# A fused embedding, attention and expert kernel: DVE's statistics of a tile behind the maximum of their unit, and one product in the next unit

## The chip, the core and the metric

The kernel runs on one core of a Trainium2 chip. The metric is the device time of one execution in microseconds (us). Three runs of the kernel before took 1317.76, 1317.83 and 1319.64 us.

The engines are named as in the profile: PE multiplies matrices, DVE, ACT and POOL work on vectors, SP issues transfers. Each runs its own list of instructions in order. They wait for one another only through semaphores, and what stands behind a waiting instruction on the same engine waits too.

## The reference, cut to what matters

Tokens (8 sequences of 1024) are hashed into 2-, 3- and 4-grams and embedded; the embedding is projected to 128 channels (`h`). Then comes attention with three branches, and then 32 experts. The change is in the attention:

```
out_cross = ln(softmax(q k_down^T) v_down)      # 512 keys: the sequence halved by a convolution
out_dot   = ln(softmax(q k^T) v)                # 1024 keys
out_cos   = ln(softmax(qn kn^T / t) v)          # 1024 keys, q and k divided by their norms
gate = softmax(concat(out_cross, out_dot, out_cos) gw + gb)
h    = h + gate0 * out_cross + gate1 * out_dot + gate2 * out_cos
```

Each `ln` subtracts a mean, divides by a standard deviation, multiplies with a weight `g` of 128 channels and adds a bias `b`. Behind this the 32 experts take the 256 tokens each that the router's softmax ranks highest, and their weighted results are added up.

## The kernel before

The attention is cut into units. A unit is one branch of one tile of 128 tokens: 8 sequences of 8 tiles with 3 branches are 192 units, and unit s belongs to the cross branch when s mod 3 is 0, to the dot branch when it is 1, to the cosine branch when it is 2. Every engine walks the same loop over s (`for s in range(N + TAIL)`), each with work of several units at once. In pass s:

- PE multiplies queries and keys of unit s into `scores`, turns the exponentials of unit s - 1 (line 610, "turned" or "mixed" <- probs) and multiplies the turned ones of unit s - 2 with the values (line 629, `mixed`). Before and behind this it computes the "items" that a table places in the pass.
- DVE copies the result of unit s - 3 out of PSUM (line 868, `o`), copies items out, and takes the row maximum of unit s (line 862, `neg_max`).
- ACT copies items, takes the exponentials of unit s (line 1019) and copies what PE turned (line 1028, `pT`).

Between these stands the work of a tile n, whose units are 3n to 3n + 2:

- pass 3n + 5: DVE's statistics (`tile_stats`, three `bn_stats` and three `bn_aggr`, lines 875 and 880), and POOL's `tile_rstd` (lines 1118 to 1126), whose third instruction waits for them;
- pass 3n + 6: DVE's `tile_gate_logits` (lines 886 to 891), which waits for `tile_rstd`;
- pass 3n + 7: ACT's exponential of the gate (line 1009), at the head of its pass; DVE's `tile_gate`: three small instructions (lines 896 to 900) and three products `u` = o * gate_r * ln_g (line 905);
- pass 3n + 8: POOL's `tile_sum` (lines 1132 to 1144): five instructions, of which the first two need the gate, and the third and later ones the products `u`. The last writes `h1`;
- pass 3n + 9: DVE's `tile_h1_stats` (lines 913 and 916), which waits for `h1` and stands ahead of the logits of the tile n + 1;
- pass 3n + 10: POOL's `tile_rstd2`, and in pass 3n + 11 ACT's `tile_x2`.

The items prepare the next sequence. Their places in the 24 passes of a sequence stand in tables: `FIRST` and `SECOND` for sequences 0 and 1, `STEADY` for sequences 2 to 6, `LAST` for 7. `|` parts what stands ahead of PE's turning from what stands behind its product with the values; a `+` means the next sequence. Two entries of `STEADY` matter here, at places 10 and 16 of 24:

```
"xT1+ | route1-"       # place 10: transposes the normalised tokens of the next sequence's second half
"k_c0+ | gram1++"      # place 16: transposes the normalised cosine keys
```

Both need POOL and another engine two passes ahead. For `xT1+`, POOL's pass of place 8 has `token_rstd` (lines 1099 to 1104), and ACT's pass of place 8 ends with `normalise` (line 1033, `xn`), which waits for it. For `k_c0+`, POOL's pass of place 14 has `cos_norm` (lines 1108 and 1111), and DVE's pass of place 15 ends with `cos_scale` (lines 794 to 801), which waits for it. In POOL's list both stand behind `tile_sum` and `tile_rstd` of their pass, since 8 and 14 are 2 modulo 3. POOL also issues the gathers of the embeddings (line 1090), three for an item, four passes ahead of it.

Of the kernel before, what the change touches and what calls it, by code (L numbers as in the profile page):

```python
# [5 lines left out]
ALU = mybir.AluOpType  # L6
# [9 lines left out]
B, S, C = 8, 1024, 128  # L16
# [19 lines left out]
BR = 3  # L36
# [71 lines left out]
N = B * UNITS  # L108
# [32 lines left out]
def items_at(s):  # L141
    return (*PLACED.get((s, 0), ()), *PLACED.get((s, 1), ()))
# [32 lines left out]
def build_program(nc, x_tok, emb, weights, cols, rows, consts, cand_bits, w_up, b_up, w_down, out):  # L175
    table = nc.dram_tensor("token_table", (TOK, XW), F32, kind="Internal").ap()
    with ExitStack() as ctx:
# [3 lines left out]
        def sem(name):  # L181
            return ctx.enter_context(nc.semaphore(name))
# [3 lines left out]
        def asb(name, shape, dt=F32):  # L186

            return attn.enter_context(nc.sbuf_tensor(name, shape, dt))
# [80 lines left out]
        o = asb("o", [P, 4, BR, VW])  # L269
# [10 lines left out]
        gate_r = asb("gate_r", [P, 2, 3])  # L280
        u = asb("u", [P, 2, BR, C])
# [54 lines left out]
        gate_r_ok = sem("gate_r_ok")  # L336
        scale_ok = sem("scale_ok")
        u_ok = sem("u_ok")
        z_g = sem("z_g")
        h1_ok = sem("h1_ok")  # L340
# [22 lines left out]
        def R(name):  # L363
            return row[:, ROW[name][0]:ROW[name][1]]
# [291 lines left out]
        def _(dve):  # L656
# [202 lines left out]
            def maxima(n):  # L859
                width = SD if n % BR == 0 else S  # L860
                dve.wait_ge(scored, n + 1)
                dve.tensor_reduce(neg_max[:, n % 4:n % 4 + 1], scores[:, (n % 2) * S:(n % 2) * S + width], AX_X,  # L862
                                  ALU.max, negate=True).then_inc(maxed, 1)

            def output(n):
                t, br = n // BR, n % BR
                dve.wait_ge(pv_done, n + 1)
                dve.tensor_copy(o[:, t % 4, br, :], mixed[:, 0:VW]).then_inc(o_ok, 1)  # L868

            def tile_stats(n):  # L870

                m = n % 2
                dve.wait_ge(o_ok, BR * n + BR)
                for br in range(BR):
                    last = dve.bn_stats(st[:, m, br, :], o[:, n % 4, br, 0:C])
                last.then_inc(o_stats, 1)
                dve.wait_ge(o_stats, n + 1)
                dve.nop(nofuse=True)
                for br in range(BR):
                    last = dve.bn_aggr(mv[:, m, br, :], st[:, m, br, :])  # L880
                last.then_inc(o_mv, 1)
# [11 lines left out]
            def tile_gate(n):  # L893
                m = n % 2
                dve.wait_ge(gate_ok, n + 1)
                dve.reciprocal(gate_inv[:, m:m + 1], gate_sum[:, m:m + 1]).then_inc(gate_c, 1)
                dve.wait_ge(gate_c, n + 1)
                dve.scalar_tensor_tensor(out=gate_r[:, m, :], in0=gate_e[:, m, :], scalar=gate_inv[:, m:m + 1],
                                         in1=rstd[:, m, :], op0=ALU.mult, op1=ALU.mult).then_inc(gate_r_ok, 1)
                dve.tensor_scalar(gate[:, m, :], gate_e[:, m, :], gate_inv[:, m:m + 1], None, ALU.mult).then_inc(scale_ok, 1)  # L900
                dve.wait_ge(gate_r_ok, n + 1)
                if n >= 2:
                    dve.wait_ge(h1_ok, n - 1)
                for br in range(BR):
                    last = dve.scalar_tensor_tensor(out=u[:, m, br, :], in0=o[:, n % 4, br, 0:C],  # L905
                                                    scalar=gate_r[:, m, br:br + 1], in1=R("ln_g")[:, br * C:(br + 1) * C],
                                                    op0=ALU.mult, op1=ALU.mult)
                last.then_inc(u_ok, 1)

            def tile_h1_stats(n):  # L910
                m = n % 2
                dve.wait_ge(h1_ok, n + 1)
                dve.bn_stats(st2[:, m, :], h1[:, n % NT, :]).then_inc(st2_ok, 1)
                dve.wait_ge(st2_ok, n + 1)
                dve.nop(nofuse=True)
                dve.bn_aggr(mv2[:, m, :], st2[:, m, :]).then_inc(mv2_ok, 1)
# [5 lines left out]
            for s in range(N + TAIL):  # L922
                if 0 <= s - 3 < N:
                    output(s - 3)
                if s % BR == 2 and 0 <= s - 5 < N:
                    tile_stats((s - 5) // BR)
                for k in PLACED.get((s - 1, 1), ()):
                    evict(k)
                if s < N:
                    maxima(s)  # L930
                for k in PLACED.get((s, 0), ()):
                    evict(k)
                if s % BR == 0 and 0 <= s - 9 < N:
                    tile_h1_stats((s - 9) // BR)
                if s % BR == 0 and 0 <= s - 6 < N:
                    tile_gate_logits((s - 6) // BR)
                if s % BR == 1 and 0 <= s - 7 < N:
                    tile_gate((s - 7) // BR)
                for where in range(2):
                    for k in PLACED.get((s - 1 - where, where), ()):  # L940
                        if ITEMS[k][0] == "route":
                            route_probs(*ITEMS[k][1:])
                for k in items_at(s + 1):
                    name, seq, j = ITEMS[k]
                    if name == "k_c" and j == 0:
                        cos_scale(seq)
# [135 lines left out]
        def _(pool):  # L1082
# [30 lines left out]
            def tile_rstd(n):  # L1113

                m = n % 2
                pool.wait_ge(exped, BR * n + BR)
                s = exp_sum[:, n % 4, :]
                pool.tensor_tensor(sum_sq[:, m, :], s, s, ALU.mult).then_inc(rstd_g, 1)
                pool.wait_ge(rstd_g, n * 3 + 1)
                pool.nop(nofuse=True)  # L1120
                pool.tensor_scalar(var_eps[:, m, :], sum_sq[:, m, :], LN_EPS, None, ALU.mult).then_inc(rstd_g, 1)
                pool.wait_ge(rstd_g, n * 3 + 2)
                pool.wait_ge(o_mv, n + 1)
                pool.tensor_tensor(var_eps[:, m, :], var_eps[:, m, :], mv[:, m, :, 1], ALU.add).then_inc(rstd_g, 1)
                pool.wait_ge(rstd_g, n * 3 + 3)
                pool.tensor_tensor(rstd[:, m, :], var_eps[:, m, :], m_half[:, 0:BR], ALU.pow).then_inc(rstd_ok, 1)

            def tile_sum(n):

                m, t, b = n % 2, n % NT, n // NT  # L1130
                pool.wait_ge(scale_ok, n + 1)
                pool.tensor_tensor(zb[:, m, :, :], R("ln_b").rearrange("p (i c) -> p i c", c=C),  # L1132
                                   gate[:, m, :].unsqueeze(2).to_broadcast([P, BR, C]), ALU.mult).then_inc(z_g, 1)
                pool.wait_ge(z_g, n * 4 + 1)
                pool.tensor_tensor(zb[:, m, 0, :], zb[:, m, 0, :], h[:, (b % 2) * NT + t, :], ALU.add).then_inc(z_g, 1)
                pool.wait_ge(z_g, n * 4 + 2)
                pool.wait_ge(u_ok, n + 1)
                pool.tensor_tensor(u[:, m, :, :], u[:, m, :, :], zb[:, m, :, :], ALU.add).then_inc(z_g, 1)  # L1138
                pool.wait_ge(z_g, n * 4 + 3)
                pool.tensor_tensor(u[:, m, 0, :], u[:, m, 0, :], u[:, m, 1, :], ALU.add).then_inc(z_g, 1)  # L1140
                pool.wait_ge(z_g, n * 4 + 4)
                if t % 4 == 0 and b > 0:
                    pool.wait_ge(h1_stored[t // 4], b * 16)
                pool.tensor_tensor(h1[:, t, :], u[:, m, 0, :], u[:, m, 2, :], ALU.add).then_inc(h1_ok, 1)
# [33 lines left out]
            for s in (2, 3):  # L1178
                for k in items_at(s):
                    if ITEMS[k][0] == "gram":  # L1180
                        gathers(*ITEMS[k][1:])
            for s in range(N + TAIL):
                if s % BR == 2 and 0 <= s - 8 < N:
                    tile_sum((s - 8) // BR)
                if s % BR == 2 and 0 <= s - 5 < N:
                    tile_rstd((s - 5) // BR)
                if s % BR == 1 and 0 <= s - 10 < N:
                    tile_rstd2((s - 10) // BR)
                for k in items_at(s + 2):
                    name, seq, j = ITEMS[k]  # L1190
                    if name == "xT":
                        token_rstd(seq, j)
                    if name == "k_c" and j == 0:
                        cos_norm(seq)
                for k in items_at(s + 4):
                    name, seq, j = ITEMS[k]
                    if name == "gram" and j < NT:
                        gathers(seq, j)
# [644 lines left out]
```

## Time and profile before

| | |
|---|---|
| median of three runs | 1317.83 us |
| the profiled execution | 1317.56 us |
| its span in the trace | 1315.6 us |
| PE busy | 1090.7 us (83%) |
| DVE busy | 832.2 us (63%) |
| POOL busy | 802.2 us (61%) |
| ACT busy | 677.2 us (51%) |
| attention, from the first maximum of scores to the last statistics of `h1` | 72.6 to 999.6 us |

The profiled execution took 1.96 us more than the span that the trace shows of it, and 0.27 us less than the median. A timeline row gives start and duration of an instruction, or of several equal ones in a row (x3), and in brackets how long the engine had been idle and who ended this. Instructions of DVE overlap a little, so that a group can be shorter than its members together.

### The profile page before, as it was taken

How to read it: one execution, taken by the hardware profiler on the slowest of the kernel's cores; microseconds unless marked ns; L12 is line 12 of the kernel's file. 1: busy time of each engine (PE TensorE's matmuls, PEld its weight loads, DVE VectorE, ACT ScalarE, POOL GpSimd, SP SyncE). 2: the span in 40 equal slices, each digit the busy share in tenths (PEclk: the TensorE clock that was granted, in tenths of full speed). 3: DMA queues.
4: the chain of work that ended last, by engine and by line, in shares of the span. 5: the costliest groups of instructions: out<-in, count | busy, mean ns of one | idle time of the engine just before them, and what ended most of it. 6: DMA issues, size and time to landing. Idle time of an engine off the chain costs nothing. (4 is left out here: it accounts for less than half of the span.)

```text
span 1315.6 us, 23060 instructions
## 1 busy us (share of the span) xinstructions
PE 1090.7 (83%) x7468; PEld 959.8 (73%) x7468; DVE 832.2 (63%) x2531; ACT 677.2 (51%) x1702; POOL 802.2 (61%) x1252
## 2 busy tenths in 40 slices
PE   3679999999999999999999999999982248876752
PEld 3569888888888988898888889888881126664541
DVE  4356777787776867777686777776675874421110
ACT  0346656666575665656566665656562543421210
POOL 5356775777467658756765775554553006778784
PEclk9889999999999999999999999999996557898885
DMA  2010001000001001100100110000002002444442
GB/s 94 22 31 25 21 20 31 25 26 18 20 24 32 27 12 43 30 9 26 31 24 14 43 29 9 11 9 19 11 9 71 0 0 48 78 94 78 83 68 23
DMA packets 49082, 42.47 MB, mean 32 GB/s; under 512 B 6728, under 2 KB 44488, under 8 KB 48840
## 3 DMA queue, kind: packets, MB, share of 16 engines
q0 software_dynamic: 18432, 22.04, 8.9%
q1 hardware_dynamic: 30536, 19.00, 4.7%
q8 instruction: 61, 1.00, 0.3%
q14 instruction: 53, 0.43, 0.1%
HBM read 27.38 MB, written 13.63 MB: 31 GB/s over the span
## 5 line engine op out<-in xcount | busy, mean ns | idle before, releaser
L629 PE MATMUL mixed<-v,pT 128*128 128x132 f32 x2560 | 320.6, 276 | 1.4 <-DVE o L868 1.4
L629 PEld LDWEIGHTS mixed<-v,pT 128*128 128x128 f32 x2560 | 302.7, 190 | 3.0 <-issue 2.6
L1090 POOL DMA_INDIRECT gram<-in_emb,ids x192 | 192.2, 1001 | 66.2 <-issue 52.7
L862 DVE TENSOR_REDUCE neg_max<-scores 128x1 f32<-128x1024 f32 (+1 forms) x192 | 199.0, 1036 | 52.0 <-PE scores L431 51.6
L1019 ACT ACTIVATE probs<-scores,neg_max 128x1024 f32<-128x1024 f32 (+1 forms) x192 | 186.7, 972 | 60.4 <-DVE neg_max L862 60.3
L1028 ACT ACTIVATE pT<-turned 128x512 f32<-128x512 f32 x211 | 125.3, 594 | 64.9 <-PE turned L610 64.5
L610 PE MATMUL turned<-con,probs 128*128 128x128 f32 x844 | 124.8, 276 | 20.0 <-ACT probs L1019 8.1
L1132 POOL TENSOR_TENSOR zb<-row,gate 128x384 f32<-128x384 f32 x64 | 54.7, 854 | 142.0 <-DVE gate L900 141.6
L429 PE MATMUL scores<-k_hi,q_hi 128*128 128x512 f32 x320 | 135.9, 425 | 2.3 <-DVE q_lo L764 2.3
L431 PE MATMUL scores<-k_hi,q_lo 128*128 128x512 f32 x320 | 126.2, 394 | 0.0
L430 PE MATMUL scores<-k_lo,q_hi 128*128 128x512 f32 x320 | 126.1, 394 | 0.0
L1779 POOL DMA_INDIRECT out_h<-yw,slots x64 | 102.2, 1597 | 36.5 <-issue 15.5
L610 PEld LDWEIGHTS turned<-con,probs 128*128 128x128 f32 x844 | 96.8, 141 | 36.8 <-ACT probs L1019 16.7
L1770 POOL DMA_INDIRECT xg<-token_table,slots x64 | 64.9, 1015 | 94.2 <-DVE slots L1632 75.0
L1729 ACT ACTIVATE hid<-scores,bup 114x256 f32<-114x256 f32 (+1 forms) x96 | 38.6, 472 | 130.8 <-PE scores L1476 130.8
L905 DVE SCALAR_TENSOR_TENSOR u<-o,gate_r,row 128x128 f32<-128x128 f32 x192 | 99.1, 570 | 0.0
L868 DVE COPY o<-mixed 128x132 f32<-128x132 f32 x192 | 54.9, 286 | 54.0 <-PE mixed L629 53.8
L1476 PE MATMUL scores<-xT,wu 128*114 128x256 f32 (+1 forms) x192 | 64.2, 483 | 24.0 <-DVE xT L1647 17.7
L1028 ACT ACTIVATE pT<-mixed 128x512 f32<-128x512 f32 x109 | 64.9, 595 | 28.9 <-PE mixed L610 28.9
L1654 DVE TENSOR_SCALAR yw<-mixed,xg 128x128 f32<-128x128 f32 x64 | 19.5, 346 | 90.1 <-PE mixed L1487 75.2
L610 PE MATMUL mixed<-con,probs 128*128 128x128 f32 x436 | 66.4, 275 | 11.6 <-ACT probs L1019 7.1
L1138 POOL TENSOR_TENSOR u<-u,zb 128x384 f32<-128x384 f32 x64 | 64.5, 1008 | 15.1 <-DVE u L905 13.7
(300 smaller groups left out, 2426.4 us busy)
## 6 DMA issues: line engine op xcount, KB each, us to landing
wd<-in_w_down SPq DMA_DIRECT2D x32, 171.0 KB
token_table<-w SPq DMA_DIRECT2D x16, 320.0 KB, 2.4
out_h<-h SPq DMA_DIRECT2D x16, 256.0 KB, 2.3
gram<-in_emb,ids POOLq DMA_INDIRECT x192, 2.6
wu<-in_w_up SPq DMA_DIRECT2D x8, 170.5 KB, 4.0
w<-in_weights SPq DMA_DIRECT2D x1, 1174.0 KB, 7.4
xg<-token_table,slots POOLq DMA_INDIRECT x64, 2.8
out_h<-yw,slots POOLq DMA_INDIRECT x64, 3.4
```

The lines of the kernel that those rows point to most:

```text
L429: pe.matmul(dst, lhs[0], rhs[0], start=first_one, stop=False)
L430: pe.matmul(dst, lhs[0], rhs[1], start=False, stop=False)
L431: return pe.matmul(dst, lhs[1], rhs[0], start=False, stop=last_one)
L610: last = pe.transpose(dst[:, j * P:(j + 1) * P], probs[:, n % 2, half * 512 + j * P:half * 512 + (j + 1) * P], ident)
L629: last = pe.matmul(mixed[:, 0:VW], pT[:, n % 2, j * P:(j + 1) * P], vals, start=(j == 0), stop=(last_half and j == half * 4 + 3))
L862: dve.tensor_reduce(neg_max[:, n % 4:n % 4 + 1], scores[:, (n % 2) * S:(n % 2) * S + width], AX_X, ALU.max, negate=True).then_inc(maxed, 1)
L905: last = dve.scalar_tensor_tensor(out=u[:, m, br, :], in0=o[:, n % 4, br, 0:C], scalar=gate_r[:, m, br:br + 1], in1=R("ln_g")[:, br * C:(b ...
L1019: act.activation(probs[:, n % 2, 0:width], scores[:, (n % 2) * S:(n % 2) * S + width], ACT.Exp, bias=neg_max[:, n % 4:n % 4 + 1], accum_ou ...
L1028: act.activation(pT[:, n % 2, half * 512:half * 512 + 512], shared_bank(TURNED_ON[n, half]), ACT.Identity).then_inc(pT_ok, 1)
L1090: pool.indirect_dma_start(gram[:, t % 4, g, :], None, emb[g], bass.IndirectOffsetOnAxis(ap=ids[:, s, t, g:g + 1], axis=0)).then_inc(gather ...
L1770: pool.indirect_dma_start(xg[:, e % XB, half, :], None, table, bass.IndirectOffsetOnAxis(ap=slots[:, k:k + 1], axis=0)).then_inc(x_in[e % ...
L1779: pool.indirect_dma_start(rows_out, bass.IndirectOffsetOnAxis(ap=slots[:, k:k + 1], axis=0), yw[:, e % EB, half, :], None, compute_op=ALU. ...
```

## The change

On DVE, `tile_stats` moves from ahead of the maximum of its pass (and of the items of the pass before) to behind it. Of the three products `u`, the first two stay behind the gate in pass 3n + 7, and the third moves into pass 3n + 8, behind the statistics of the next tile. Each product now signals `u_ok`, and POOL waits for three signals a tile. On POOL, `tile_rstd` of the tile n and `tile_sum` of the tile n - 1, which stand in one pass, change places.

```
@@ vector: tile_gate ends behind tensor_scalar(gate...)
-                dve.wait_ge(gate_r_ok, n + 1)
-                if n >= 2:
-                    dve.wait_ge(h1_ok, n - 1)
-                for br in range(BR):
-                    last = dve.scalar_tensor_tensor(out=u[:, m, br, :], in0=o[:, n % 4, br, 0:C],
-                                                    scalar=gate_r[:, m, br:br + 1], in1=R("ln_g")[:, br * C:(br + 1) * C],
-                                                    op0=ALU.mult, op1=ALU.mult)
-                last.then_inc(u_ok, 1)
+            def tile_gain(n, br):
+                m = n % 2
+                if br == 0:
+                    dve.wait_ge(gate_r_ok, n + 1)
+                    if n >= 2:
+                        dve.wait_ge(h1_ok, n - 1)
+                dve.scalar_tensor_tensor(out=u[:, m, br, :], in0=o[:, n % 4, br, 0:C],
+                                         scalar=gate_r[:, m, br:br + 1], in1=R("ln_g")[:, br * C:(br + 1) * C],
+                                         op0=ALU.mult, op1=ALU.mult).then_inc(u_ok, 1)
@@ vector: the loop
-                if s % BR == 2 and 0 <= s - 5 < N:
-                    tile_stats((s - 5) // BR)
                 for k in PLACED.get((s - 1, 1), ()):
                     evict(k)
                 if s < N:
                     maxima(s)
+                if s % BR == 2 and 0 <= s - 5 < N:
+                    tile_stats((s - 5) // BR)
...
                 if s % BR == 1 and 0 <= s - 7 < N:
                     tile_gate((s - 7) // BR)
+                    tile_gain((s - 7) // BR, 0)
+                    tile_gain((s - 7) // BR, 1)
+                if s % BR == 2 and 0 <= s - 8 < N:
+                    tile_gain((s - 8) // BR, 2)
@@ gpsimd: tile_sum
-                pool.wait_ge(u_ok, n + 1)
+                pool.wait_ge(u_ok, n * BR + BR)
@@ gpsimd: the loop
+                if s % BR == 2 and 0 <= s - 5 < N:
+                    tile_rstd((s - 5) // BR)
                 if s % BR == 2 and 0 <= s - 8 < N:
                     tile_sum((s - 8) // BR)
-                if s % BR == 2 and 0 <= s - 5 < N:
-                    tile_rstd((s - 5) // BR)
```

On DVE, in the passes of places 7 to 9 of a sequence, there stood before (`gate_r` and `gate` are the end of `tile_gate`, `st<-o` and `mv<-st` the statistics, `neg_max` the maxima of places 8 and 9, `st<-h` and the `mv` behind it `tile_h1_stats`):

```order
L900 TENSOR_SCALAR gate<-gate_e,gate_inv 128x3
L905 SCALAR_TENSOR_TENSOR u<-o,gate_r,row 128x128 x3
L868 COPY o<-mixed 128x132
L875 BN_STATS st<-o 128x6 x3
L880 BN_AGGR mv<-st 128x2 x3
L862 TENSOR_REDUCE neg_max<-scores 128x1
L868 COPY o<-mixed 128x132
L862 TENSOR_REDUCE neg_max<-scores 128x1
L913 BN_STATS st<-h 128x6
L916 BN_AGGR mv<-st 128x2
L886 TENSOR_TENSOR logit<-o,rstd 128x3x3
```

In the changed kernel there stands at the same place of DVE:

```order
L900 TENSOR_SCALAR gate<-gate_e,gate_inv 128x3
L908 SCALAR_TENSOR_TENSOR u<-o,gate_r,row 128x128 x2
L868 COPY o<-mixed 128x132
L862 TENSOR_REDUCE neg_max<-scores 128x1
L875 BN_STATS st<-o 128x6 x3
L880 BN_AGGR mv<-st 128x2 x3
L908 SCALAR_TENSOR_TENSOR u<-o,gate_r,row 128x128
L868 COPY o<-mixed 128x132
L862 TENSOR_REDUCE neg_max<-scores 128x1
L915 BN_STATS st<-h 128x6
L918 BN_AGGR mv<-st 128x2
L886 TENSOR_TENSOR logit<-o,rstd 128x3x3
```

The maximum of place 8 moved ahead of the statistics, and the third product behind them. Nothing was added or taken away.

On POOL, in the pass of place 8, there stood before (`zb` to `h` is `tile_sum`, `sum_sq` to `rstd` is `tile_rstd`, and the last row is the first of `token_rstd`):

```order
L1132 TENSOR_TENSOR zb<-row,gate 128x384
L1135 TENSOR_TENSOR zb<-zb,h 128x128
L1138 TENSOR_TENSOR u<-u,zb 128x384
L1140 TENSOR_TENSOR u<-u 128x128
L1144 TENSOR_TENSOR h<-u 128x128
L1118 TENSOR_TENSOR sum_sq<-exp_sum 128x3
L1121 TENSOR_SCALAR var_eps<-sum_sq 128x3
L1124 TENSOR_TENSOR var_eps<-var_eps,mv 128x3
L1126 TENSOR_TENSOR rstd<-var_eps,m_half 128x3
L1099 TENSOR_SCALAR shift<-mv 128x4
```

In the changed kernel (lines from here on are 6 higher):

```order
L1124 TENSOR_TENSOR sum_sq<-exp_sum 128x3
L1127 TENSOR_SCALAR var_eps<-sum_sq 128x3
L1130 TENSOR_TENSOR var_eps<-var_eps,mv 128x3
L1132 TENSOR_TENSOR rstd<-var_eps,m_half 128x3
L1138 TENSOR_TENSOR zb<-row,gate 128x384
L1141 TENSOR_TENSOR zb<-zb,h 128x128
L1144 TENSOR_TENSOR u<-u,zb 128x384
L1146 TENSOR_TENSOR u<-u 128x128
L1150 TENSOR_TENSOR h<-u 128x128
L1105 TENSOR_SCALAR shift<-mv 128x4
```

The two groups changed places; what comes behind both kept its place. At place 14 it is the same, with `cos_norm` behind both groups:

```order
L1132 TENSOR_TENSOR rstd<-var_eps,m_half 128x3
L1138 TENSOR_TENSOR zb<-row,gate 128x384
L1141 TENSOR_TENSOR zb<-zb,h 128x128
L1144 TENSOR_TENSOR u<-u,zb 128x384
L1146 TENSOR_TENSOR u<-u 128x128
L1150 TENSOR_TENSOR h<-u 128x128
L1114 TENSOR_TENSOR norm<-norm,p_half 128x16
```

This is the changed kernel; before, `cos_norm` followed `tile_rstd` there.

## Rows read from the trace of the kernel before

**Rows 1.** Busy time by stage: stretch, us, then each engine, PEclk, DMA share, GB/s.

```profile
79.60:89.70 10.10, 6.91 (x26) 5.29 (x25) 5.07 (x8) 3.41 (x7) 7.97 (x8) 0.50 0.19 50
600.00:800.00 200.00, 192.98 (x1412) 175.95 (x1411) 150.40 (x442) 124.79 (x306) 140.14 (x243) 1.00 0.10 28
```

**Rows 2.** PE's waits from 60 to 1005 us: total, times, longest.

```profile
PE turned L610 <- ACT probs L1019: 8.1, 9, 1.9
PE mixed L610 <- ACT probs L1019: 7.1, 9, 1.1
```

**Rows 3.** Timeline of DVE, units 128 and 129: start us, us, instruction [idle before].

```profile
699.27 1.72 DVE L905 SCALAR_TENSOR_TENSOR u<-o,gate_r,row 128x128 f32<-128x128 f32 x3
...
701.23 0.68 DVE L875 BATCH_NORM_STATS2 st<-o 128x6 f32<-128x128 f32 x3
...
702.24 1.19 DVE L862 TENSOR_REDUCE neg_max<-scores 128x1 f32<-128x1024 f32 x1
...
704.18 0.28 DVE L913 BATCH_NORM_STATS2 st<-h 128x6 f32<-128x128 f32 x1
```

**Rows 4.** Line 905 as a whole: shortest, median and longest of one, in ns.

```profile
L905 DVE SCALAR_TENSOR_TENSOR u<-o,gate_r,row x192: 336/495/1657, 115.2 to 996.2; 128x128 f32<-128x128 f32 x192
```

**Rows 5.** Timeline of POOL, units 128 and 129.

```profile
699.44 0.86 POOL L1132 TENSOR_TENSOR zb<-row,gate 128x384 f32<-128x384 f32 x1 [3.98 <-DVE gate L900]
...
702.76 0.46 POOL L1144 TENSOR_TENSOR h<-u 128x128 f32<-128x128 f32 x1
...
703.86 0.20 POOL L1124 TENSOR_TENSOR var_eps<-var_eps,mv 128x3 f32<-128x3 f32 x1
704.13 0.89 POOL L1126 TENSOR_TENSOR rstd<-var_eps,m_half 128x3 f32<-128x3 f32 x1
...
706.84 0.20 POOL L1104 TENSOR_TENSOR shift<-shift,rstd 128x4 f32<-128x4 f32 x1
```

**Rows 6.** Timeline of PE, units 128 to 130.

```profile
700.68 0.39 PE L431 MATMUL scores<-k_hi,q_lo 128*128 128x512 f32 x1
...
704.73 0.66 PE L610 MATMUL mixed<-con,probs 128*128 128x128 f32 x4 [0.75 <-ACT probs L1019]
...
709.75 0.66 PE L489 MATMUL mixed<-con,xn 128*128 128x128 f32 x4 [0.68 <-ACT pT L1028]
```

**Rows 7.** Timeline of ACT, unit 128's end.

```profile
707.08 1.65 ACT L1033 ACTIVATE xn<-h,shift,rstd 128x128 f32<-128x128 f32 x4 [1.92 <-POOL shift L1104]
```

**Rows 8.** Timeline of DVE, units 134 to 138.

```profile
732.16 1.21 DVE L862 TENSOR_REDUCE neg_max<-scores 128x1 f32<-128x1024 f32 x1
...
738.27 2.41 DVE L801 TENSOR_TENSOR qk_raw<-qk_raw,inv_norm 128x1024 f32<-128x1024 f32 x2
...
756.10 0.17 DVE L886 TENSOR_TENSOR logit<-o,rstd 128x9 f32<-128x9 f32 x1 [1.24 <-POOL rstd L1126]
```

**Rows 9.** Timeline of POOL, units 134 to 137.

```profile
734.28 2.92 POOL L1108 TENSOR_TENSOR norm<-norm,p_half 128x16 f32<-128x16 f32 x1
...
754.20 0.19 POOL L1118 TENSOR_TENSOR sum_sq<-exp_sum 128x3 f32<-128x3 f32 x1
```

**Rows 10.** Timeline of PE, units 136 and 139.

```profile
740.09 0.60 PE L532 MATMUL mixed<-con,qk_raw 128*128 128x128 f32 x4
...
757.00 2.04 PE L629 MATMUL mixed<-v,pT 128*128 128x132 f32 x16 [0.18 <-DVE o L868]
```

**Rows 11.** Timeline of DVE, the last sequence and its end.

```profile
957.90 1.19 DVE L862 TENSOR_REDUCE neg_max<-scores 128x1 f32<-128x1024 f32 x1
...
963.32 0.30 DVE L868 COPY o<-mixed 128x132 f32<-128x132 f32 x1 [2.06 <-PE mixed L629]
...
993.61 0.17 DVE L886 TENSOR_TENSOR logit<-o,rstd 128x9 f32<-128x9 f32 x1 [1.22 <-POOL rstd L1126]
```

**Rows 12.** Timeline of PE, the last sequence.

```profile
964.93 1.97 PE L629 MATMUL mixed<-v,pT 128*128 128x132 f32 x16
```

**Rows 13.** Timeline of PE, the start of the first sequence.

```profile
79.24 0.84 PE L532 MATMUL mixed<-con,qk_raw 128*128 128x128 f32 x4 [3.48 <-DVE qk_raw L801]
```

## The prediction, made before the changed kernel had run

> **What bounds the kernel now.** I read the busy time by stage first. In the steady part PE is busy 192.98 of 200 us at a granted clock of 1.00, the full 2.4 GHz [rows 1]; DVE, ACT and POOL have 50 to 75 us of rest each. So the attention lasts as long as PE's list, and only what makes PE wait or stops making it wait counts. Then I read PE's waits: 18 of them, 15.2 us in all, are for ACT's exponentials [rows 2], and ACT in turn waited for DVE's maximum. The timeline shows the pattern. The scores of unit 128, a cosine unit, are ready at 701.07 (start plus duration of PE's last product of them), PE gets to the turning of unit 128 and stands 0.75 us [rows 6], because DVE starts the maximum only at 702.24, behind the statistics that began at 701.23 [rows 3]. That is what the change goes for.
>
> Then I read who waits for POOL. ACT's `normalise` of the next sequence's tokens waited 1.92 us for the last instruction of `token_rstd` and began at 707.08, when that ended at 707.04 [rows 5, 7]. PE transposed the result at 709.75, as soon as ACT had copied one more tile [rows 6]. So this chain had no reserve at all: POOL, ACT, PE. At place 14 `cos_norm` began at 734.28 [rows 9], DVE's scaling with its result at 738.27 [rows 8], two halves in 2.41 us, so the first half was done at 739.5, and PE took it at 740.09 [rows 10]: 0.6 us of reserve.
>
> **The change, part by part.** The maximum of each cosine unit no longer stands behind the statistics: 1.0 us from 701.23 to 702.24 [rows 3], so it starts when its scores are ready, at 701.1 in this place. PE's waits of rows 2 go: at most 15.2 us. A good part of these lies at the five places like unit 128 (0.75 us each), in the last sequence and in the drain, which are worked out whole below. For the rest and some copies of items that DVE then makes earlier I take 8 us as gain, with 3 and 15 as ends.
>
> The products: three took 1.72 us together at 699.27 [rows 3], the shortest single one 0.336 [rows 4]. The first ran alone, the other two beside POOL's `zb` at 699.44 and the addition behind it [rows 5]. Now POOL does not begin `zb` there, since `tile_rstd` stands ahead, so two products end behind 0.6 us. DVE has rest there, so this gives PE nothing beyond the above; the third, 0.34 to 1.7 us [rows 4], stands ahead of a cross maximum and costs nothing, because POOL reaches the addition that needs it only later.
>
> Now POOL, which is the price. Before, `tile_sum` of the tile n - 1 ran from 699.44 to 703.22 [rows 5], while DVE made the products and the statistics; POOL had been idle 3.98 us before it. In the new order it is behind `tile_rstd` of the tile n, which waits for the statistics, which are behind the maximum. From the start of the maximum:
> - maximum 1.2, statistics 1.1 (0.1 more than their lead of 1.0 in rows 3);
> - the part of `tile_rstd` behind the statistics: from 703.86 to 705.02, 1.2 us [rows 5];
> - `tile_sum`: 3.78 less the 0.29 that it waited for a product, 3.5 us.
>
> That is 7.0 us from the start of the maximum to `h1`. On DVE `tile_h1_stats` waits for it and the logits stand behind: 1.0 us more (from 704.18 on it was the same work), 8.0 in all.
>
> Place 1, units 128 to 130: `tile_sum` ends at 701.1 + 7.0 = 708.1. `token_rstd`, behind both groups before and after, takes 2.0 us (705.02 to 707.04, [rows 5]), ends at 710.1 and not at 707.04: 3.1 us later. ACT's `normalise` waits in order, and its copies and exponentials stand behind it; PE's transposes start at 712.8 and not at 709.75. The 0.75 us that PE won just before are lost again in this wait. Net +3.1 us for each of the five sequences 2 to 6: 15.5 us. In the first sequence the same item stands at the same place; PE takes it with more reserve, 2 us (0 to 3). Sequence 1 has it two places later: 0.
>
> Place 2, units 134 to 139: the maximum at 732.16 [rows 8] can start up to 0.8 us earlier, at 731.4, so `tile_sum` ends at 738.4 and `cos_norm` starts then and not at 734.28 [rows 9]: 4.1 us later. The first half of the scaling ends at 743.6, and PE's transposes move from 740.09 to 743.65: 3.6 us. Behind `cos_norm` POOL had no rest until 754.24, where `tile_sum` of place 17 ended (six gathers, `tile_rstd2`, three gathers); all of it is 4.1 us late. There `tile_rstd` steps ahead too, 1.9 us from 754.20 to about 756.1 [rows 8, 9]. So `h1` comes at 760.2, the logits end at 761.2 and not at 756.6, and DVE's copy of a result, for which PE's products at 757.00 waited already [rows 10], comes 4.6 us later. Net +4.6 us, 3.6 if POOL's queue eases: five times, 23 us.
>
> At the other places 7.0 us is a wait of DVE at `tile_h1_stats`, of 0 to 4 us: at unit 129 DVE was there at 704.18 [rows 3], `h1` will come at 708.1. DVE's next copy has to wait for PE anyway, as it did 2.06 us at 963.32 [rows 11], so I take this at 0, except in the last sequence, whose tiles are short. There the maximum at 957.90 would start at 957.0, the logits end at 965.0, and the copy that ran at 963.32 [rows 11] ends at 965.3; PE's products that need it started at 964.93 [rows 12]. Each of seven tiles gets 0.4 us longer (-0.5 to +1): 3 us. In the drain nothing hides the chain of the last tile: its logits stood at 993.61 [rows 11] behind `tile_sum` and `tile_rstd`. By the pattern of place 1 `tile_sum` ends 4.9 us later (708.1 against 703.22, [rows 5]), and `tile_rstd` with its 1.9 us no longer stands between it and the logits: +3 us.
>
> Sum: 15.5 + 2 + 23 + 3 + 3 - 8 = +38.5 us. The profiled execution took 1317.6, so 1356; the median of the runs is 0.3 higher. At place 1 PE would stand idle from 708.3 to 712.8 (its scores ended at 709.07 before, less 0.75). After an idle time of 3.48 us [rows 13] the granted clock was 0.50, or 1.2 GHz, from 79.6 to 89.7 [rows 1], so such a fall may follow here. If each of ten long waits cost 1 to 3 us in this way, that would be 10 to 30 us. I take 4 us as a part of it, and forecast 1360.
>
> The Trainium skill, "TensorE: Matmul & The Clock Gate", in the section on HAM oscillation, says that a gap in PE's work that is long enough sends the clock back to half rate and that the matmuls behind it pay. Its figure for one gap (1.67 us at half rate, half of it lost) would add about 8 us over ten gaps, 1364 in all; that is an estimate from the page. The trace agrees in that the clock fell behind 3.48 us of idle time [rows 13, 1] and stayed at 1.00 in the steady part; it does not show what a gap of 4.5 us inside the dense part does.
>
> **The rivals.**
> - Faster: the waits of rows 2 go, and POOL's later sum is taken up by rest. For it: POOL was idle 3.98 us before `tile_sum` [rows 5] and busy only 70% [rows 1]. Against it: `normalise` began 0.04 us behind POOL's last instruction [rows 5, 7]. It decides at `token_rstd`: if that still ends by 707 us, PE gains. Then -15 us of rows 2 and 3 of item copies, 1300. Chance 0.07.
> - Gains and losses cancel, within 0.2% (2.6 us, about what a measurement of this kernel tells from no change): losses only at place 1, the gain 15. Chance 0.03.
> - Slower, but only half: place 1 costs 15.5, place 2 little, since its stages move together and PE has reserve; 15.5 + 3 + 4 - 8, 1332. For it: 0.6 us of reserve before 740.09, and the gathers' items may come in time. Chance 0.15.
> - Much slower: the clock falls at both places, and DVE's waits of up to 4 us at `tile_h1_stats` delay the copies of items, so that PE waits for PSUM banks: 38 + 20 + 5, 1381. Chance 0.2.
> - The forecast, 1345 to 1370. Chance 0.55.
>
> The range reaches from the half case to the much slower one: 1332 to 1384. Slower by over 0.2%: 0.55 + 0.15 + 0.2 = 0.90; faster 0.07; within 0.2% 0.03.
>
> **What would show each step.** In the changed kernel's timeline: the cosine maximum starts within 0.1 us of its scores; the first two products take 0.6 us and meet no `zb`; PE's waits for exponentials behind a cosine unit are gone; in their place POOL's `zb` starts about 3.5 us behind the start of the maximum, DVE waits at the statistics of `h1` for POOL in most tiles, ACT's `xn` waits about 5 us for POOL's last `shift` of a half sequence, and PE waits 4 us at the transposes of `xn` and 3 to 4 us at those of the scaled `qk_raw`. A sequence of the steady part takes 6 to 9 us longer. The forecast is wrong if `tile_sum` ends less than 6 us behind the start of the maximum, or if ACT's `xn` does not wait, and its size is wrong if the granted clock falls below 1.00 in many places.

## The result, and the profile of the changed kernel

The changed kernel takes 1378.83 us (median of 4 runs, 1377.14 to 1380.72) beside 1317.89 for the kernel before on the same chip: ratio 1.0451, 95% interval 1.0434 to 1.0469. The forecast was 1360, with a range of 1332 to 1384. The profiled execution took 1378.11 us with a span of 1376.2. From line 898 on ACT's and POOL's lines stand 6 higher; the product is line 908. A ratio here can differ from the quotient of the two medians beside it by up to 0.2 points.

Busy time by stage, as in [rows 1], of the changed kernel:

```profile
600.00:800.00 200.00, 180.59 (x1274) 167.46 (x1274) 125.67 (x400) 113.25 (x279) 124.22 (x218) 0.95 0.09 24
...
738.07:744.88 6.81, 6.01 (x29) 6.01 (x29) 1.94 (x7) 4.73 (x12) 0.18 (x1) 0.50 0.02 4
```

PE is busy 180.6 of 200 us and not 193, and the granted clock is 0.95: it fell to 0.50, which is 1.2 GHz, for instance from 738.07 on. PE's waits from 60 to 1062 us, beside [rows 2]:

```profile
PE mixed L489 <- ACT pT L1034: 24.0, 5, 4.8
PE mixed L532 <- DVE qk_raw L801: 20.8, 6, 4.0
PE mixed L629 <- DVE o L868: 17.8, 16, 3.9
...
PE turned L610 <- ACT probs L1025: 0.8, 1, 0.8
PE mixed L610 <- ACT probs L1025: 0.2, 1, 0.2
```

The waits for exponentials are gone (1.0 us of 15.2). The new ones are those for the normalised tokens (L489, place 10 of the table, the prediction's "place 1") and for the scaled cosine queries and keys (L532, place 16, the prediction's "place 2"; 3.5 of the 20.8 us stood at the kernel's start before too, [rows 13], and the fifth wait of the steady part, 4.3 us, is under `turned`). By sequence: 4.81 us at place 10 (0.68 to 0.70 before) and 3.96 to 4.26 us at place 16 (none to 0.19 before) in each of sequences 2 to 6.

Place 10 on DVE, answering [rows 3]; the numbers at the end are idle time and its releaser:

```profile
727.13 1.22 DVE L862 TENSOR_REDUCE neg_max<-scores 128x1 f32<-128x1024 f32 x1 [1.02 <-PE scores L431]
728.27 0.67 DVE L875 BATCH_NORM_STATS2 st<-o 128x6 f32<-128x128 f32 x3
729.04 0.32 DVE L880 BATCH_NORM_AGGREGATE mv<-st 128x2 f32<-128x6 f32 x3
729.27 0.32 DVE L908 SCALAR_TENSOR_TENSOR u<-o,gate_r,row 128x128 f32<-128x128 f32 x1
...
734.19 0.29 DVE L915 BATCH_NORM_STATS2 st<-h 128x6 f32<-128x128 f32 x1 [3.80 <-POOL h L1150]
```

The same place on POOL, answering [rows 5]:

```profile
729.50 0.20 POOL L1130 TENSOR_TENSOR var_eps<-var_eps,mv 128x3 f32<-128x3 f32 x1 [5.56 <-DVE mv L880]
729.78 0.89 POOL L1132 TENSOR_TENSOR rstd<-var_eps,m_half 128x3 f32<-128x3 f32 x1
730.64 0.83 POOL L1138 TENSOR_TENSOR zb<-row,gate 128x384 f32<-128x384 f32 x1
...
733.70 0.46 POOL L1150 TENSOR_TENSOR h<-u 128x128 f32<-128x128 f32 x1
...
735.97 0.20 POOL L1110 TENSOR_TENSOR shift<-shift,rstd 128x4 f32<-128x4 f32 x1
```

ACT there, answering [rows 7], and then PE, answering [rows 6]:

```profile
736.21 1.65 ACT L1039 ACTIVATE xn<-h,shift,rstd 128x128 f32<-128x128 f32 x4 [6.13 <-POOL shift L1110]
```

```profile
738.87 1.11 PE L489 MATMUL mixed<-con,xn 128*128 128x128 f32 x4 [4.81 <-ACT pT L1034]
```

Read it as one chain. The maximum starts at 727.13, POOL stands 5.56 us until the statistics behind it are there, then does `tile_rstd`, the whole `tile_sum` (h1 at 734.16, 7.0 us behind the start of the maximum) and `token_rstd`. ACT waits 6.13 us for its last instruction and PE stands 4.81 us. PE's four transposes then take 1.11 us, not 0.66, at the fallen clock.

### The profile page after: what moved, and what is told of

The parts are those of the page before. It is cut to its first block and busy times, and to the rows that moved or that the text cites. A ratio compares the mean times of both kernels' runs of the same rounds, so it can differ in the third digit from the quotient of the medians.

```text
span 1376.2 us, 23060 instructions
## 1 busy us (share of the span) xinstructions
PE 1112.4 (81%) x7468; PEld 988.6 (72%) x7468; DVE 779.0 (57%) x2531; ACT 678.3 (49%) x1702; POOL 796.6 (58%) x1252
## 5 line engine op out<-in xcount | busy, mean ns | idle before, releaser
L629 PE MATMUL mixed<-v,pT 128*128 128x132 f32 x2560 | 338.0, 286 | 19.3 <-DVE o L868 17.8
L629 PEld LDWEIGHTS mixed<-v,pT 128*128 128x128 f32 x2560 | 319.9, 199 | 22.8 <-issue 20.5
L1130 POOL TENSOR_TENSOR var_eps<-var_eps,mv 128x3 f32<-128x3 f32 x64 | 12.7, 198 | 257.0 <-DVE mv L880 256.0
L610 PEld LDWEIGHTS turned<-con,probs 128*128 128x128 f32 x844 | 102.7, 146 | 13.1 <-ACT probs L1025 2.3
L1735 ACT ACTIVATE hid<-scores,bup 114x256 f32<-114x256 f32 (+1 forms) x96 | 38.5, 471 | 132.6 <-PE scores L1482 132.6
L915 DVE BATCH_NORM_STATS2 st<-h 128x6 f32<-128x128 f32 x64 | 18.7, 292 | 144.9 <-POOL h L1150 144.9
L431 PEld LDWEIGHTS scores<-k_hi,q_lo 128*128 128x128 f32 x320 | 60.4, 189 | 14.3
L1482 PEld LDWEIGHTS scores<-xT,wu 128*114 128x114 f32 (+1 forms) x192 | 40.0, 223 | 40.6 <-DVE xT L1653 22.8
```

The costliest lines, as they stand in the source:

```text
L431: return pe.matmul(dst, lhs[1], rhs[0], start=False, stop=last_one)
L610: last = pe.transpose(dst[:, j * P:(j + 1) * P], probs[:, n % 2, half * 512 + j * P:half * 512 + (j + 1) * P], ident)
L629: last = pe.matmul(mixed[:, 0:VW], pT[:, n % 2, j * P:(j + 1) * P], vals, start=(j == 0), stop=(last_half and j == half * 4 + 3))
L1482: last = pe.matmul(up_bank[0:n, c * TOPK:(c + 1) * TOPK], wu[:, g % 2, c * FP:c * FP + n], xT[:, e % 2, :], start=True, stop=True)
```

## The experiments

The change has three parts: S, the statistics behind the maximum; D, the third product in the next pass; P, POOL's `tile_rstd` ahead of `tile_sum`. The runs do them alone and in pairs. "h1" and "rstd" are worked out from each trace: time from the start of a cosine maximum to the end of POOL's `tile_sum` and `tile_rstd` of that pass, median over tiles 2 to 59. The two waits are PE's at places 10 and 16 of sequence 4. "at 0.50" is the time at a granted clock of 0.50 from unit 3 to unit 191, and "last" the time from the scores of unit 168 to those of unit 191, the last sequence, all in us. Chips differ (the kernel before takes 1318, 1337 or 1344 us), so only ratios to the kernel before on the same chip are compared.

| kernel | parts | ratio, 95% interval | h1 | rstd | PE at 10 / 16 | at 0.50 | last |
|---|---|---|---|---|---|---|---|
| before | none | 1 | 0.7 | 2.5 | 0.7 / 0 | 0 | 92.4 |
| e2b_stats_alone | S | 0.9900 (0.9881-0.9919) | 1.7 | 3.6 | 1.7 / 0.6 | 6.8 | 85.5 |
| e3b_pool_alone | P | 1.0024 (1.0009-1.0038) | 4.6 | 1.1 | 2.8 / 1.5 | 13.7 | 85.8 |
| e9_product_and_pool | D, P | 1.0019 (1.0002-1.0035) | 4.9 | 1.0 | 2.7 / 1.3 | 17.1 | 85.5 |
| e4b_product_alone | D | 1.0254 (1.0231-1.0277) | 4.5 | 6.3 | 3.3 / 3.4 | 54.6 | 88.2 |
| e1b_pool_back | S, D | 1.0307 (1.0278-1.0335) | 5.3 | 7.2 | 4.3 / 4.2 | 64.9 | 89.0 |
| e8_stats_and_pool | S, P | 1.0439 (1.0406-1.0471) | 7.0 | 3.5 | 4.8 / 4.0 | 64.9 | 98.9 |
| after | S, D, P | 1.0451 (1.0434-1.0469) | 7.0 | 3.5 | 4.8 / 4.0 | 61.4 | 98.9 |

**Going back one part, and each part alone (four runs, one chip).** The expectations in us were made for a kernel before of 1318 us; on this chip it took 1337.47, so each is read as a ratio. The first is the changed kernel with POOL's order of before:

```
-                    tile_rstd((s - 5) // BR)      # ahead of tile_sum
+                    tile_rstd((s - 5) // BR)      # behind tile_sum
```

> Edit: the changed kernel with POOL's two blocks in the order of before (tile_sum ahead of tile_rstd); DVE as changed. Theory 'late sum' (POOL's chain from the cosine maximum to h1 and to the next rstd is what PE ends up waiting for, and the third product holds it as much as POOL's order does): tile_sum still waits for the third product, about 4 us behind the start of the cosine maximum, so h1 comes at about 6 us and rstd behind it at about 8; the tokens' rstd1 is as late as in the changed kernel, PE's idle at place 10 stays at 4 to 5 us: 1365 to 1385. Rival 'POOL's order alone': with the order back the time is back too: 1305 to 1325.

Measured 1380.13 us beside 1337.47, ratio 1.031. POOL now waits inside `tile_sum`, for the third product, and `tile_rstd` is held behind it. One row of POOL's waits (total, times, longest):

```profile
POOL u L1144 <- DVE u L908: 183.1, 50, 6.4
```

The rival is out: putting the order back does not bring the time back. But the ratio is 1.4 points below that of the full change, and below the 1.036 to 1.051 of the expectation. The table shows where about half of that lies: h1 comes at 5.3 us and not at 7.0, and the last sequence takes 89.0 us and not 98.9 (97.3 in the changed kernel's trace on a third chip). In that sequence PE waits for DVE's copies of o, which stand behind h1.

Statistics alone (`tile_stats` behind `maxima`, nothing else):

> Edit: the kernel before with tile_stats behind the maximum and nothing else; three products in one pass and POOL's order as before. Theory 'late sum': h1 comes as early as before, rstd about 1.8 us later than before; PE's 15 us of waits for exponentials go, places 10 and 16 get 1.8 us longer each in five sequences (18 us), no fall of the clock because no wait passes 3 us: 1310 to 1325. Rival 'the statistics' move is the cost': most of the 61 us is here, 1350 or more.

Measured 1324.28 us, ratio 0.990: the moved statistics alone are a gain, and more of one than expected (0.994 to 1.005). `tile_sum` stands ahead, with its inputs early, and POOL does it in the time in which it would wait for the statistics anyway. PE's waits for exponentials fall to 1.0 us, and its waits at the two places are short (3.5 us of the second row are the kernel's start). The expectation had the clock fall nowhere; it fell once, for 3.4 us in sequence 6 behind a wait of 1.7 us at place 10:

```profile
PE mixed L489 <- ACT pT L1028: 8.5, 5, 1.7
...
PE mixed L532 <- DVE qk_raw L801: 6.7, 6, 3.5
```

POOL's order alone (two blocks swapped in the kernel before):

> Edit: the kernel before with POOL's order swapped (tile_rstd ahead of tile_sum) and nothing else. Theory 'late sum': tile_sum can start only behind rstd, h1 comes about 4 us later than before and the tokens' rstd1 about 2 us: places 10 and 16 get some 2 us longer, DVE waits at tile_h1_stats: 1335 to 1355. Rival 'POOL's order costs nothing while POOL has idle time': 1315 to 1322.

Measured 1340.16 us, ratio 1.002. That is the rival's number and not the theory's 1.013 to 1.028, but not the rival's reason: the waits came (2.8 and 1.5 us at the two places), and something paid for them: the waits for exponentials went, and the last sequence took 85.8 us and not 92.4. The product shows why the exponentials came sooner. POOL no longer runs `zb` beside the three products. DVE's product as a group (busy time and mean ns of one):

```profile
L905 DVE SCALAR_TENSOR_TENSOR u<-o,gate_r,row 128x128 f32<-128x128 f32 x192 | 56.6, 350 | 0.0
```

In the kernel before the same row says 99.1 us and 570 ns. With DVE free 0.7 us sooner in these passes (three of 350 ns, not of 570), the waits for exponentials fell to 1.3 us, with no change in the place of the statistics. So most of the 15 us of [rows 2] could be had in either way.

The third product alone:

> Edit: the kernel before with the third product moved into the next pass and nothing else (statistics ahead of the maximum, tile_sum ahead of tile_rstd). Theory 'late sum': the third product comes behind the maximum, so h1 and all behind it on POOL are some 2.5 us later than before: places 10 and 16 longer by that: 1335 to 1355. Rival 'the third product is free to move': 1310 to 1322, the 1.1 us of DVE in the pass before being a gain.

Measured 1372.31 us, ratio 1.025, within the theory's 1.013 to 1.028. The product sits behind a maximum, POOL waits for it with `tile_sum` at the head of its queue, and `tile_rstd`, whose inputs are long there, comes at 6.3 us instead of 2.5. POOL at unit 101, and then DVE's product:

```profile
606.95 1.02 POOL L1144 TENSOR_TENSOR u<-u,zb 128x384 f32<-128x384 f32 x1 [3.95 <-DVE u L908]
...
609.96 0.89 POOL L1132 TENSOR_TENSOR rstd<-var_eps,m_half 128x3 f32<-128x3 f32 x1
```

```profile
606.48 0.32 DVE L908 SCALAR_TENSOR_TENSOR u<-o,gate_r,row 128x128 f32<-128x128 f32 x1
```

**Pairs with POOL's new order.** Statistics and POOL, the product back:

> Edit: the kernel before with the statistics behind the maximum and POOL's two blocks swapped; the three products stay in one pass. Theory 'late sum': with the swap tile_sum stands behind rstd, and rstd waits for the statistics; so h1 is as late as in the changed kernel though the third product is early, and the place-10 wait is 4 to 5 us: ratio 1.035 to 1.045. Rival 'the edits add up' (statistics alone 0.990, swap alone 1.002): 0.99 to 1.00.

Measured 1378.70 us beside 1318.47, ratio 1.044: the whole loss, without the product. The parts alone would add up to 0.992. DVE waits for h1 as in the changed kernel, and PE's row for L489 is the same to a tenth:

```profile
611.83 0.29 DVE L913 BATCH_NORM_STATS2 st<-h 128x6 f32<-128x128 f32 x1 [3.91 <-POOL h L1144]
```

```profile
PE mixed L489 <- ACT pT L1028: 24.0, 5, 4.8
```

Product and POOL, the statistics ahead again:

> Edit: the changed kernel with the statistics ahead of the maximum again; the third product in the next pass, POOL's blocks swapped. Theory 'late sum': rstd is done before the third product, the chain behind it is no later than with the product alone (1.025): 1.020 to 1.030, and the wait at place 10 about 3 us. Rival 'the edits add up': 1.027 plus.

Measured 1321.73 us, ratio 1.002: better than either theory said. `tile_rstd` has its inputs and leaves at once, so the late product holds nothing but the sum, which has to make `zb` first anyway:

```profile
584.50 0.20 POOL L1130 TENSOR_TENSOR var_eps<-var_eps,mv 128x3 f32<-128x3 f32 x1 [5.36 <-DVE mv L880]
...
588.69 0.45 POOL L1150 TENSOR_TENSOR h<-u 128x128 f32<-128x128 f32 x1
```

DVE's maximum started at 584.27 there, with the statistics before it. What follows from the table: a part costs time only where it makes the input of the block late that stands first in POOL's queue. With `tile_sum` first the late product costs 2.5 to 4 points (D against none, S with D against S); with `tile_rstd` first it costs nothing (D with P against P; after against S with P), and there the late statistics cost 4.2 to 4.3. By the later of the two ends, h1 or rstd, the ratios are: 3.6 us 0.990, 4.6 and 4.9 us 1.002, 6.3 us 1.025, 7.2 us 1.031, 7.0 us 1.044 and 1.045 (the kernel before, 2.5 us, has the waits for exponentials instead). The last three are out of order by that measure. Part of the reason is that h1 counts by itself in the last sequence: in the changed versions with h1 at up to 4.9 us it took 85.5 to 88.2 us, at 5.3 us 89.0, and at 7.0 us 98.9. Statistics and POOL together (1378.7 us) against product and POOL (1321.7) is the plainest pair, as both ran on one chip: of 58.0 us between their spans 31.7 lie in sequences 2 to 6, 13.4 in the last, 6.7 in the first.

**The changed kernel again, and `token_rstd` and `cos_norm` ahead of `tile_sum`.**

> The changed kernel itself once more, beside the others, because chips differ (the kernel before took 1318 us on one and 1337 on another). Every theory: the ratio to before that was measured first, 1.043 to 1.047, if ratios carry over between chips; 1.03 to 1.04 if the half-clock stretches that this chip already gives the kernel before take a part of the difference.

Measured 1403.55 us beside 1344.14 on a third chip: ratio 1.0433 (1.0402 to 1.0465). The ratio carries over between chips, the time does not: this trace is 26.7 us longer than that of the same kernel on the first chip.

> Edit: the changed kernel with token_rstd and cos_norm between tile_rstd and tile_sum on POOL. Theory 'late sum': tile_sum (3.5 us) no longer stands ahead of what PE waits for, so PE's waits at place 10 and 16 fall from 4.8 and 4.0 to 1.3 and 0.5 us and the clock does not fall behind them; h1 comes 2 to 3 us later at these two places only: 25 to 40 us faster than the changed kernel (1338 to 1354 beside its 1379). Rival 'DVE's wait for h1': the wait at tile_h1_stats grows by what the tokens' chain gains, holds DVE's next copies of o and PE behind them: within 10 us of the changed kernel.

Measured 1384.53 us, ratio 1.0294 (1.0261 to 1.0326), 19 us less than the changed kernel, between the two expectations (25 to 40 us, and under 10). Each theory is right at one place. At place 10 PE's wait fell to 1.3 us. At place 16 of sequence 4 it grew from 4.1 to 5.4 (3.6 to 5.4 in sequences 2 to 5): `cos_norm` is ready, but DVE's scaling stands in its queue behind `tile_h1_stats`, and h1 is now behind `cos_norm`. DVE, then PE:

```profile
658.52 0.29 DVE L915 BATCH_NORM_STATS2 st<-h 128x6 f32<-128x128 f32 x1 [5.78 <-POOL h L1150]
...
660.35 2.36 DVE L801 TENSOR_TENSOR qk_raw<-qk_raw,inv_norm 128x1024 f32<-128x1024 f32 x2
```

```profile
661.72 1.09 PE L532 MATMUL mixed<-con,qk_raw 128*128 128x128 f32 x4 [5.36 <-DVE qk_raw L801]
```

**Extra products in PE's waits, to price the clock (two runs).** The changed kernel with

```
+                for _ in range(count):        # 36 ahead of xT 1, 30 ahead of k_c 0
+                    pe.matmul(scores[:, at:at + 256], w_hi[:, 0:P], w_hi[:, 0:256], ...)
```

> Edit: the changed kernel with extra products on PE in front of its two long waits (36 of 256 columns ahead of xT 1, 30 ahead of k_c 0, for the items of sequences 3 to 7), whose result is overwritten unread; they fill some 4 us and 3.4 us of waits of 4.8 and 4.0 us. Theory 'the fall of the clock costs by itself': the granted clock stays 1.00 behind places 10 and 16 (51 of 61 us at 0.50 go) and 13 to 20 us come back, though nothing that PE waits for comes sooner. Rival 'the waits alone are the cost, the half clock falls where PE has time': within 4 us of the changed kernel or, if the extra products delay PE, some us slower.

Measured 1424.95 us beside 1344.14, ratio 1.0595. It missed what it was for: these products wait for the exponential of the last unit, and that stands on ACT behind `normalise`, the very thing PE waits for. So they came behind the wait and ran at the fallen clock (36 in 6.93 us):

```profile
645.34 6.93 PE L561 MATMUL scores<-w_hi 128*128 128x256 f32 x36 [5.49 <-ACT probs L1035]
```

The second run writes them to unused columns of `mixed` instead, behind the copy of o alone:

> Edit: the changed kernel with extra products on PE in its two long waits, as in the run with 66 of them, but now behind no wait for an exponential (they write columns 256 to 511 of mixed, which nobody reads, and wait only for the copy of o two units back). Theory 'the fall of the clock costs by itself': the clock stays 1.00 behind places 10 and 16, 10 to 20 us less than the changed kernel: ratio 1.030 to 1.037. Rival 'the waits are the whole cost': 1.043 to 1.047, or above where the extra products reach past the wait.

Measured 1393.81 us beside 1318.47, ratio 1.0566 (1.0532 to 1.0600), slower again. Its rows of PE at the two places:

```profile
620.34 4.57 PE L560 MATMUL mixed<-w_hi 128*128 128x256 f32 x36 [1.41 <-DVE o L877]
624.75 0.60 PE L489 MATMUL mixed<-con,xn 128*128 128x128 f32 x4
...
659.75 5.42 PE L560 MATMUL mixed<-w_hi 128*128 128x256 f32 x29 [5.28 <-DVE o L877]
```

At place 16 even the copy of o is behind DVE's scaling, so the extra products came behind 5.28 us of idle time and ran mostly at half clock, and the unit took 15.88 us, where the changed kernel took 11.82. At place 10 it worked. The clock stayed at 1.00, and PE went from its first transpose to the next scores in 3.49 us (624.75 to 628.24) where the changed kernel took 4.97 (615.62 to 620.59) in the same sequence. So the wait's end and the 3.4 us at half clock behind it cost 1.5 us together. The kernel before took 3.77 us there, behind a wait of 0.68 us at the full clock: 0.3 us of the 1.5 is what a wait costs beside its idle time, and 1.2 the clock. This run lost 1.0 of the 1.5 again by reaching past the wait. The total does not decide between the theories; the place does.

**A version that beats both.** The kernel before with S alone, and on POOL `token_rstd` and `cos_norm` between `tile_sum` and `tile_rstd`, where POOL had waited for the statistics (`tile_rstd2` moves behind them too):

```
                 tile_sum((s - 8) // BR)
+                token_rstd / cos_norm of items_at(s + 2)
                 tile_rstd((s - 5) // BR)
```

> Edit: the kernel with only the statistics moved behind the maximum (its ratio was 0.990) and, on POOL, token_rstd and cos_norm ahead of tile_rstd, in the time in which POOL waits for the statistics. Theory 'POOL's chain sets PE's waits': the wait at place 10 (1.7 us) and what is left at place 16 (0.8 us) go, the gate's rstd comes 1 to 2 us later at these places and nobody on PE waits for it: ratio 0.980 to 0.987. Rival 'late gate': DVE waits at tile_gate_logits for what was gained: ratio 0.989 to 0.995 or worse.

Measured 1314.03 us beside 1344.14, ratio 0.9771 (0.9740 to 0.9802), below what was expected. PE's wait at place 10 is gone and no fall of the clock is left in sequences 1 to 6; the wait at place 16, expected to go too, stayed at 0.6 to 0.8 us. The price is where the rival put it, on DVE, and nobody on PE waits for it. POOL's end of `token_rstd`, then DVE's logits:

```profile
709.47 0.20 POOL L1104 TENSOR_TENSOR shift<-shift,rstd 128x4 f32<-128x4 f32 x1
```

```profile
711.50 0.17 DVE L886 TENSOR_TENSOR logit<-o,rstd 128x9 f32<-128x9 f32 x1 [2.30 <-POOL rstd L1126]
```

**The kernel before, for its trace.**

> The kernel before itself, for its trace on a chip on which it takes 1337 to 1344 us and not 1318. Theory: the 20 us are in the first sequence and in the experts' part, and in no wait of sequences 2 to 6. Rival: they are spread over all sequences, and then ratios of this chip speak of another balance.

It ran on a chip on which it takes 1318 us (one run, 1317.73), so for this kernel the other chips' 20 us stay open. The changed kernel has traces on two of the chips, and between them its span differs by 26.7 us: 12.7 of these come before the scores of unit 24 (one wait of 5.1 us at unit 3 among them), and 14.3 in sequences 2 to 6, of which 12.7 at places 14 and 18. So for that kernel sequences 2 to 6 do take a part, which speaks for the rival. PE's waits for the low parts of the queries at place 14, in `a_again`; the trace on the first chip has no such row:

```profile
PE turned L610 <- DVE q_lo L769: 7.8, 4, 2.0
```

What makes them late on that chip stays open. The waits and lengths of the other variants traced on the slower chips can hold a share of this; their ratios are each taken on one chip.

## Why the prediction was right, and where its sizes were off

**The mechanism.** It was as forecast, within 0.3 us where the chain was worked out: h1 at 7.0 us behind the start of the maximum (forecast 7.0), the first two products in 0.61 us (0.6), PE's idle time at place 10 4.81 us (4.5), DVE's wait at h1 3.8 us (4), a steady sequence 6.3 to 9.4 us longer (6 to 9). That the later end in POOL's queue is the cause is shown by the table, above all by S with P. But the prediction priced the edits as one chain and did not say that S alone is a gain; the runs add that.

**The sum.** Measured against its terms, by the starts of the scores in both traces (the span grew by 60.6 us, the sum said 38.5 and 4 for the clock). "Length" is the time from one unit's scores to the next:
- Sequences 2 to 6: +41.0 us, forecast 15.5 + 23 - 8 + 4 = 34.5. The lengths by place give each term, five sequences together:
  - Place 1 of the prediction: PE waits 20.6 us more at place 10, and place 9 is 5.1 us shorter. That is 15.5, as forecast, but two misses of 0.27 us a sequence cancel: PE waits 4.12 us more and not 3.85, and place 9 is shorter by 1.02 and not by 0.75.
  - Place 2: 20.0 us more of waiting at place 16 (forecast 18), and -0.2 at place 19, where the forecast had 5.
  - The gain: all other places together are 14.0 us shorter, within the 3 to 15 of the prediction but not the 8 that it took. This is what is left after new waits for DVE's copies of o at places 1 and 22 (+4.7 and +1.0 us of length), behind `tile_h1_stats`, a wait that the prediction put at 0 outside the last sequence.
  - The clock: places 10 and 16 grew by 8.6 and 11.1 us beyond their waits, 19.7 in all, with ten falls and 51 us at 0.50. In sequence 4 it was 1.2 us for a fall of 3.4 us and 2.7 us for one of 6.8. Up to 1.4 of the 11.1 can be what any wait costs beside its idle time, since there was none at place 16 before. The prediction's own bounds were 10 to 30, and it took 4 "as a part of it": this is the term that it sized worst. The kernel before had no such stretch between units 3 and 191, so only the 3.48 us at its start [rows 13] spoke for it, and that row should have been taken at its word.
- The first sequence +4.9 (forecast 2): at place 10 PE waits 2.7 us more and the clock falls there too, for 6.8 us; that place alone is 5.8 us longer. The last sequence +6.6 (3): there DVE's copies of o are late in nearly every tile (L629, 0.6 to 2.1 us each), with one fall of 3.4 us.
- Behind unit 191: +9.0 (3). PE's wait for the last tile grew from 5.8 to 8.6 us as forecast, but a wait of 3.9 us for the last copies of o is new. The prediction followed the last tile only, not the one before it. PE's waits of the changed kernel from 1026 to 1115 us:

```profile
PE turned L538 <- ACT w L1047: 8.6, 1, 8.6
...
PE mixed L629 <- DVE o L868: 5.0, 2, 3.9
```

These make the 18 us between 1360 and the profiled 1378, to the tenths lost in rounding: 6.5, 2.9, 3.6 and 6.0, less 0.5 in sequence 1 and 0.3 before the first unit.

**The rivals.** "Faster" and "cancel" were out from place 10 on. "Half" is out: place 16 costs as much as place 10. "Much slower" named 1381 with falls at both places, which is what the clock did; its other cause, PE waiting for PSUM banks, did not show. The measured 1378.8 lies nearer to its 1381 than to the forecast of 1360, though not by its sum: the waits cost no more than forecast, and the clock and the gain were both sized too small. The estimate from the Trainium skill, "TensorE: Matmul & The Clock Gate", section on HAM oscillation, was 8 us for ten gaps; the traces show ten falls of 3.4 or 6.8 us behind the long waits inside the dense part, 19.7 us in all.

## What to carry to other kernels

On an engine that works in order, put the block first whose inputs are ready first; before moving a producer, ask which block at the head of each consumer's queue waits for it, and what unrelated work stands behind. One move can be a gain with one order of the consumer and the whole loss with the other, so price edits as pairs, not as a sum. The time in which an engine must wait anyway is the place for work that others wait for, as POOL's `token_rstd` showed. Where the change makes TensorE wait for several us, count the slower products behind the wait as well. To price a wait, compare the starts of the work behind it in two traces, not the idle times: the waits that went here gave back about a half more than their idle time.

## What the runs showed of the hardware

- DVE's product of 128x128 f32 takes 0.34 to 0.37 us on average in the kernels with `tile_rstd` first, in which POOL's `zb` no longer runs beside the first two, and 0.56 to 0.57 in the kernels in which `zb` and POOL's additions run beside all three. Taking them apart gave back nearly as much of the waits for exponentials as moving the statistics did. The Trainium skill, "GPSIMD Engine Reference", section on specifications, says that POOL's interfaces to SBUF are shared with DVE's instructions that have two inputs in SBUF; the product has two, and the runs agree (it names no price).
- A wait of PE costs more than its idle time also at the full clock. Place 9 had a wait of 0.75 us before and none in the changed kernel, and its unit became 1.02 us shorter. Without the wait the transposes there start 0.44 us behind the start of the group ahead of them, which takes 0.60; a wait takes this overlap of 0.16 away, and two groups behind it take 0.05 us more each. Outside places 10 and 16, waits shorter by 12.7 us in five sequences went with units shorter by 19.3.
- Behind a wait of 1.7 us at place 10 the granted clock fell once (statistics alone, sequence 6), and behind the same 2.8 us at place 10 it fell in sequences 2 to 4 and not in 5 and 6 of one kernel (POOL alone). The length of the wait alone did not say whether it would fall.
- Chips differ by 2% in the kernel before (1318 to 1344 us), but the ratio of the changed kernel to it was 1.0451 on one and 1.0433 on another.
